# A graph-transformer kernel: reload, additions, norm and node projection joined in one stage by groups of five tiles

## What is computed

```python
# end of layer 0: x = x + mixture(layernorm(x)), the mixture returns tokens + shares
out = tokens                                   # the normed rows
for e in range(E):                             # 8 experts, the best two of a token count
    h = gelu(tokens @ w1[e] + b1[e]); y = h @ w2[e] + b2[e]
    out = out + combine[:, e:e + 1] * y
# start of layer 1
xn = layernorm(x)
hid = relu((xn[src] + edge_attr) @ W1 + b1)    # 40000 edges
```

## Time and profile before

| | us |
|---|---|
| median of 3 runs | 1409.33 (1406.69 to 1414.96) |
| the profiled execution | 1415.98 |
| its span | 1414.0 |
| busy PE / DVE / ACT / POOL | 1169.0 / 754.9 / 454.0 / 595.6 |
| mean granted clock of PE | 0.922 |

### The profile page before, as it was taken

One profiled execution on the slowest core, in us unless ns is written; L12 is line 12 of the kernel. 1 busy time (PEld: TensorE's weight loads), 2 busy tenths in 40 slices (PEclk: granted clock), 3 DMA queues, 4 the chain that ended last, 5 costly groups with the idle time before them and its releaser, 6 DMA issues. The chain is left out here.

```text
span 1414.0 us, 22751 instructions
## 1 busy us (share of the span) xinstructions
PE 1169.0 (83%) x7588; PEld 921.5 (65%) x7588; DVE 754.9 (53%) x2376; ACT 454.0 (32%) x916; POOL 595.6 (42%) x698
## 2 busy tenths in 40 slices
PE   3777789876972899617999999999999869966997
PEld 2677779443641677416878888888888645535886
DVE  5999981276578344384545555454356431252332
ACT  2477770331321332111324333333333233221110
POOL 3366640003121677402776676766667000003442
PEclk9899999997965899959999999999999989987999
DMA  5000000410025233365666666656565056576551
GB/s 126 1 2 2 2 2 2 107 12 1 0 71 192 78 98 99 92 161 156 199 175 191 183 198 181 188 180 190 176 192 180 6 171 186 117 159 206 172 177 53
DMA packets 97276, 165.62 MB, mean 117 GB/s; under 512 B 15506, under 2 KB 59182, under 8 KB 96774
## 3 DMA queue, kind: packets, MB, share of 16 engines
q1 hardware_dynamic: 71669, 90.69, 22.5%
q0 software_dynamic: 25488, 73.39, 17.9%
HBM read 138.40 MB, written 27.63 MB: 117 GB/s over the span
## 5 line engine op out<-in xcount | busy, mean ns | idle before, releaser
L2266 POOL DMA_INDIRECT em_gathered<-edge_table,el_which x313 | 301.7, 964 | 132.1 <-issue 74.2
L2278 PE MATMUL em_projected<-em_w,em_attr 128*128 128x256 f32 x1252 | 283.1, 384 | 7.6 <-PEq L1897 7.6
L2278 PEld LDWEIGHTS em_projected<-em_w,em_attr 128*128 128x128 f32 x1252 | 240.4, 193 | 42.5 <-issue 9.9
L2356 DVE TENSOR_TENSOR em_hidden<-em_projected,em_gathered 128x512 f32<-128x512 f32 (+1 forms) x157 | 108.3, 690 | 205.2 <-PE em_projected L2278 127.3
L2378 ACT ACTIVATE em_hidden<-em_hidden 128x512 f32<-128x512 f32 (+1 forms) x157 | 98.7, 628 | 271.5 <-DVE em_hidden L2356 271.4
L434 POOL TENSOR_SCALAR nm_hot_a<-nm_order,ek_places 128x125 bf16<-128x125 int16 x150 | 99.7, 673 | 51.1 <-PE nm_banks L558 47.7
L446 DVE TENSOR_SCALAR nm_hot_key<-nm_key_order,ek_keys 128x100 bf16<-128x100 int16 x500 | 118.4, 263 | 0.0
L2689 POOL DMA_INDIRECT oe_hidden<-oe_table,oo_node x27 | 25.9, 959 | 179.4 <-DMA oe_table<-state 130.0
L2761 PE MATMUL oe_banks<-oe_wd,xn_T 128*128 x432 | 98.1, 381 | 0.0
L445 DVE TENSOR_SCALAR nm_hot_a<-nm_order,ek_places 128x125 bf16<-128x125 int16 x350 | 94.6, 272 | 0.0
L2761 PEld LDWEIGHTS oe_banks<-oe_wd,xn_T 128*128 128x128 f32 x432 | 80.7, 192 | 9.8
(11 more groups left out here) (482 smaller groups left out, 2267.0 us busy)
## 6 DMA issues: line engine op xcount, KB each, us to landing
em_attr<-in_edge_attr_sets SPq DMA_DIRECT2D x156, 256.0 KB, 3.6
oe_table<-state SPq DMA_DIRECT2D x20, 448.0 KB
oe_wd<-in_ffn_Wd SPq DMA_DIRECT2D x8, 1024.0 KB
em_gathered<-edge_table,el_which POOLq DMA_INDIRECT x313, 3.6
mx_w<-in_ffn_w SPq DMA_DIRECT2D x16, 256.0 KB
oe_table<-state SPq DMA_DIRECT2D x1, 2248.8 KB
state<-in_x SPq DMA_DIRECT2D x5, 448.0 KB
state<-in_x SPq DMA_DIRECT2D x1, 2240.0 KB
```

What stands on the lines that cost most here:

```text
L2266: nc.gpsimd.indirect_dma_start(out=gathered[:, n % GATHERED, :], out_offset=None, in_=table, in_offset=bass.IndirectOffsetOnAxis(ap=lanes. ...
L2278: last = nc.tensor.matmul(projected[:, k % BANKS, n % 2, :], attr[:, k % ATTR_RING, (n % 2 * KB + f) * 128:(n % 2 * KB + f + 1) * 128], w1 ...
L2356: nc.vector.tensor_tensor(pair_slots(k), projected[:, k % BANKS, 0:width, :], gathered[:, at:at + width, :], ALU.add).then_inc(pre_ready, 1)
```

## The change

The reload and the additions leave the mixture's block; `normalise_to_first` becomes `answers_to_first`, which does them together with norm and projection, in four groups of five tiles (`PARTS`, `SIZE`).

- The first addition is split: ACT multiplies the first answer by its share in place (`weight`, L1972 of the changed kernel), POOL adds it to x (L1898), DVE adds the second answer as before (`add_second`, L1905).
- Statistics, variance and root are worked out per group. DVE normalises a group one group late: additions and statistics of group g, its variance, then the norm of group g - 1.
- The bias of the projection is added by PE, by a matmul of one row of ones with one row of the bias (L1949). ACT copies the projection out of PSUM (`keep`, L1980), three tiles behind the turn (L1984). DVE's copy is gone.
- SP issues the answers' loads, the attributes', the weights', clears, and only then stores the table, in four stores of five tiles.
- `hidden_sum`, which the edge stage fills later, now also takes the second answers; it, the shares and `answers` are made earlier for that.

The core of the diff (the removed lines of the mixture are L1697 to L1701 and L1854 to L1869 above, those of the old stage L1880 to L1968):

```diff
-def normalise_to_first(p, c, A, x, xn, xn_T, w, b, attr, attr_loaded, table, others, done):
+def answers_to_first(p, c, A, x, xn, xn_T, w, b, shares, answers, second, attr, attr_loaded, table, others, done):
-    BANKS, PARTS = 4, 5
+    BANKS, PARTS = 4, 4
     SIZE = TILES // PARTS
+    answer = [xn[:, :, 0:DIM], second[:]]
...
             @block.sync
             def _(sp):
+                for q in range(CHUNKS):
+                    for n in range(2):
+                        load_rows(sp, answer[n][:, q * 4:(q + 1) * 4, :],
+                                  answers[n * NODES + q * CHUNK:n * NODES + (q + 1) * CHUNK, :]
+                                  .rearrange("(t p) d -> p t d", p=P), answered[n][q])
                 for k in range(ATTR_RING):
                     load_attributes(sp, A, attr, attr_loaded, k)
-                for q in range(PARTS):
...
                 others.sync(sp)
                 clear(sp, done)
+                for g in range(PARTS):
+                    sp.wait_ge(kept, (g + 1) * SIZE)
+                    load_rows(sp, table[g * SIZE * P:(g + 1) * SIZE * P, :].rearrange("(t p) d -> p t d", p=P),
+                              rows[:, g * SIZE:(g + 1) * SIZE, :], stored)
                 sp.wait_ge(stored, 32 * PARTS)
+
+            @block.gpsimd
+            def _(pool):
+                for t in range(TILES):
+                    pool.wait_ge(weighted, t + 1)
+                    nc.gpsimd.tensor_tensor(x[:, t, :], x[:, t, :], answer[0][:, t, :], ALU.add).then_inc(joined, 1)

             @block.vector
             def _(dve):
+                def add_second(t):
+                    dve.wait_ge(answered[1][t // 4], 32)
+                    dve.wait_ge(joined, t + 1)
+                    nc.vector.scalar_tensor_tensor(x[:, t, :], answer[1][:, t, :], shares[1][:, t:t + 1], x[:, t, :],
+                                                   ALU.mult, ALU.add).then_inc(added, 1)
...
+                for g in range(PARTS):
+                    for t in tiles_of(g):
+                        add_second(t)
+                        if t % SIZE:
+                            measure(t - 1)
+                    measure(t)
+                    find_var(g)
+                    if g:
+                        normalise(g - 1)
+                normalise(PARTS - 1)
...
+                    nc.tensor.matmul(projected[:, t % BANKS, 0:DIM], c.ones[0:1, :P], b[0:1, :], start=True, stop=False)
                     for k in range(KB):
                         last = nc.tensor.matmul(projected[:, t % BANKS, 0:DIM], xn_T[:, k, t * P:(t + 1) * P], w[:, k, :],
-                                                start=(k == 0), stop=(k == KB - 1))
+                                                start=False, stop=(k == KB - 1))
...
             @block.scalar
             def _(act):
+                def weight(t):
+                    act.wait_ge(answered[0][t // 4], 32)
+                    nc.scalar.activation(answer[0][:, t, :], answer[0][:, t, :], ACT.Copy, scale=shares[0][:, t:t + 1]).then_inc(weighted, 1)
...
+                for g in range(PARTS + 2):
+                    if g < PARTS:
+                        for t in tiles_of(g):
+                            weight(t)
+                    if 1 <= g <= PARTS:
+                        root(g - 1)
+                    if g >= 2:
+                        for t in tiles_of(g - 2):
+                            turn(t)
+                for t in range(TILES - 3, TILES):
+                    keep(t)
```

More of the change, by code:

```diff
@@ L1625, in tensor_steps, with mixture @@
         last.then_inc(self.found, 1)
-def mixture(p, c, A, state, x, xn, xn_T, first_w, first_b):
+def mixture(p, c, A, state, x, xn, xn_T, first_w, first_b, shares, answers):
     nc = p.nc
@@ new lines, in measure, with find_var @@
+                def measure(t):
+                    dve.wait_ge(added, t + 1)
+                    nc.vector.bn_stats(c.stats[:, t * 6:(t + 1) * 6], x[:, t, :]).then_inc(measured, 1)
+                def find_var(g):
+                    dve.wait_ge(measured, (g + 1) * SIZE)
+                    nc.vector.tensor_tensor(half[:, g], s[:, g, 1, :], s[:, g, 4, :], ALU.subtract)
+                    nc.vector.tensor_tensor(mean[:, g], s[:, g, 1, :], s[:, g, 4, :], ALU.add)
+                    chain.tick(nc.vector.tensor_tensor(var[:, g], s[:, g, 2, :], s[:, g, 5, :], ALU.add))
+                    chain.wait(dve)
+                    nc.vector.tensor_scalar(mean[:, g], mean[:, g], 0.5, None, ALU.mult)
+                    chain.tick(nc.vector.scalar_tensor_tensor(half[:, g], half[:, g], 0.25, half[:, g], ALU.mult, ALU.mult))
+                    chain.wait(dve)
+                    chain.tick(nc.vector.scalar_tensor_tensor(var[:, g], var[:, g], 1.0 / DIM, half[:, g], ALU.mult, ALU.add))
+                    chain.wait(dve)
+                    nc.vector.tensor_scalar(var[:, g], var[:, g], LN_EPS, None, ALU.add).then_inc(var_ready, 1)
@@ L1961, in _, with root, keep, turn @@
             def _(act):
-                act.wait_ge(var_ready, 1)
-                nc.scalar.activation(std[:], var[:], ACT.Sqrt).then_inc(std_ready, 1)
-                for t in range(TILES):
+                def weight(t):
+                    act.wait_ge(answered[0][t // 4], 32)
+                    nc.scalar.activation(answer[0][:, t, :], answer[0][:, t, :], ACT.Copy, scale=shares[0][:, t:t + 1]).then_inc(weighted, 1)
+                def root(g):
+                    act.wait_ge(var_ready, g + 1)
+                    nc.scalar.activation(std[:, g], var[:, g], ACT.Sqrt).then_inc(std_ready, 1)
+                def keep(t):
+                    act.wait_ge(ready, t + 1)
+                    nc.scalar.activation(rows[:, t, :], projected[:, t % BANKS, 0:DIM], ACT.Copy).then_inc(kept, 1)
+                def turn(t):
                     act.wait_ge(transposed, t + 1)
@@ L2583, in layer1 @@
             attr_loaded = [p.sem(f"em_attr_loaded{u}") for u in range(ATTR_RING)]
[L2584 removed]
+            answers_to_first(p, c, A, x, xn, xn_T, w1, b1, shares, answers, hidden_sum, attr, attr_loaded, table, w, done)
             p.reuse(done)
@@ L2924, in graph_layers @@
         first_b = p.sb("em_b1", [P, DIM], scope=graph)
-        mixture(p, c, A, state, x, xn, xn_T, first_w, first_b)
+        hidden_sum = p.sb("hidden_sum", [P, TILES, DIM], scope=graph)
+        shares = [p.sb(f"shares{n}", [P, TILES], scope=graph) for n in range(2)]
+        answers = nc.dram_tensor("mx_answers", [2 * NODES, DIM], F32).ap()
+        mixture(p, c, A, state, x, xn, xn_T, first_w, first_b, shares, answers)
     if upto >= 3:
-        layer1(p, c, A, x, xn, xn_T, lanes, in_degree, first_w, first_b)
+        layer1(p, c, A, x, xn, xn_T, lanes, in_degree, first_w, first_b, shares, answers, hidden_sum)
 def laid_out(i):
```

73 lines of the change are left out of this document (17 added, 56 removed).

## The result

| | before | after |
|---|---|---|
| median | 1409.62 us | 1446.67 us (1445.9 to 1448.13) |
| ratio | | 1.0256, 95% interval 1.0233 to 1.028 |
| span of the profiled execution | 1414.0 | 1444.7 |
| busy PE | 1169.0 | 1215.9 |
| mean granted clock of PE | 0.922 | 0.905 |

The change made the kernel 37 us slower. The forecast was 1402.2, its range ended at 1409. Four points of each trace say where the time is: POOL's last indirect DMA of the mixture is issued, PE begins the first transpose of the stage, the last copy out of PSUM begins, the edge stage's first matmul begins.

The account below looks back on a forecast made before the run. The stretch was taken as bound in turn by loads and VectorE, TensorE, then SP's list. Gains of 4.2 us at PE's end and 2.9 at SP's made 7.1, from median 1409.33 to 1402.2 us; range 1396.5 to 1409.

Parts of the forecast that it names:

- Bias on PE: Projection: the one-row matmul adds 0.43 us, PE's tile goes from 1.08 to 1.51, taking back 8.6 us of 14.6.
- Rival C: Norm and projection: PE works in shorter pieces, its clock stays at 1.2 GHz, up to 1427.6 us; chance 0.06.
- Reload: Answers' loads move behind the mixture's block end, which costs 0.3 us; what is lost at 593 is won at 626.
- Additions: Answer additions: POOL and DVE take turns, 1.0 us a tile for the pair; PE starts at 614.6, not 629.25.
- rival A: Additions: POOL always goes before DVE, PE starts at 617.9, 2.7 us gained, 1406.6; chance 0.28 including nothing moving.
- Groups: Norm stage: group 2 is normalised from 631.4, PE has run out at 630.5, a wait of 1.3 us.
- SP's end: Last copy to edge stage: clears before stores leave 4.1 us and 0.1 of hand-over, for 7.1; 2.9 us gained.
- Sum: Mixture's end to edge stage: 7.1 us gained, 4.2 at PE's end and 2.9 at SP's; chance 0.47.

Follow-up runs that it names:

- e11: Changed kernel with the bias over 125 rows, the first two chunks loaded early and both additions on VectorE: ratio 0.9953 to the kernel before.
- e8: Changed kernel with the bias matmul over 125 rows and the first two of five chunks' loads issued inside the mixture's block: ratio 0.9958 to the kernel before.
- e2: Changed kernel with the bias matmul over 125 rows in place of one: ratio 1.0017 to the kernel before.
- e14: Changed kernel with the bias over 125 rows in tiles 0 to 9 and one row in tiles 10 to 19: ratio 1.0028 to the kernel before.
- e6: Changed kernel with the bias added by GpSimd to the copied rows, none on PE: ratio 1.0007 to the kernel before.
- e1: Changed kernel without the bias matmul, so its projection lacks the bias: ratio 0.9987 to the kernel before.
- e17: e11 with groups normalised after three tiles of the next, ScalarE's roots reordered, and 34 full-width matmuls ahead of the first transpose: ratio 0.9958 to the kernel before.
- e18: e17 with 16 more full-width matmuls behind the last projection: ratio 0.9934 to the kernel before.

## Why the prediction was wrong

*Bias on PE: the step that failed.* It says "the rows don't count, the columns do", from one 1-row record of 385 ns beside records of 384. For the duration of a lone record that is right, and with 125 rows the bias costs the 0.43 us forecast. But the row I read stood in a stage whose clock was already up, and it was one record, not one in every tile. Neither what it does to the clock, nor the steps around it (0.57 us a tile at half clock, 0.38 at full) is in such a row. Size: the bias was priced at 0.43 us a tile and cost 2.48 (3.56 less 1.08); from first transpose to last copy it was 71.5 us, forecast 35.1, and with 125 rows 34.3. Why few rows keep the clock down stays open: the runs show that they do.

*Rival C* named what came, a clock that stays at 1.2 GHz, and had 0.06 and the wrong reasons. The waits at group ends and the transposes are in the run with 125 rows too, where the clock rose; the part of its "for" that held was "one-row" matmuls. It gave the end of the last copy at 675.5; 690.93 came, 15.4 us later, of which 4.5 are the late start (619.06 against 614.6) and some 11 are 20 x 0.57. My argument against it, that the clock rose before "of the same mixture of work", was the mistake: the mixture was the one thing that the edit changed. By the rule of the Trainium skill that I weighed there (TensorE: Matmul & The Clock Gate, "PE-mode transpose"), transposes do not engage the full clock. The runs agree with the earlier trace rows and not with it: transposes and full-width projections alone, in the run without bias, had the clock at 1.00 from 3.5 us behind the first transpose.

*Reload: the other step that failed.* "One such end costs 0.3 us" was read at 626, at this very block's end, when POOL's drain had been over for 26 us. Moved to 591, the same end has the drain in it. "What is lost at 593 is won at 626" took the two for alike: 6.8 us by the trace, nearly the whole gain forecast.

*Additions.* From the first load to the first transpose 21.6 us, forecast 20.9: right. But this was luck in part: the term was argued from a collision, and that was mild. DVE's twenty additions in after took 0.46 to 0.98 us, and none the 1.5 or more that would have spoken for rival A; without any sharing, in the run e11, the first transpose comes as early (24.1 us against 25.5 from the last DMA).

*Groups.* One wait of 1.3 us at group 2: in the run e8 it is 1.03, at that place. In after PE is so slow that it doesn't occur.

*SP's end.* 4.2 us from the end of the last copy to the edge stage, measured 4.4 (690.93 to 695.37), and by itself, in the old order, 3 us of gain. Right.

*Sum.* With the bias over 125 rows and two chunks loaded early (e8) the forecast's mechanism is there: 0.9958 for 0.995, and 64.4 us from last DMA to edge stage, where the forecast's times give 63.1.

## What to carry to other kernels

Before a small matmul is put into a stage that TensorE bounds, ask how many of its rows it uses, not only how many columns it streams: here the same sum over 125 rows, all but one of them times zero, cost 0.43 us a tile, and over 1, 32 or 64 rows 2.5. When work is moved across a block's end, look at what each engine has to finish at that end, above all one that has issued its own DMAs; an end that costs 0.3 us at one place can cost 7 at another. And before reordering in-order lists, follow the whole loop through the engines: an early start that hangs weights behind turns made the period of a group longer than any engine's work.

## What the runs showed of the hardware

- Narrow matmuls (1, 32, 64 rows of contraction), two records to four full-width ones and two transposes, went with a granted clock of 0.50 for 70 us at a PE busy all the time; with 125 rows it rose, 4.1 us after the first transpose in e2. Once it was 1.00, one-row ones left it there for 17 us (e14).
- Each costs more than its columns: 0.38 us a tile at full clock, 0.57 at half.
- GpSimd's drain at the end of a block, counted from the end of its last instruction, differs with what it did there, and is the same in all twenty traces: 7.75 us at the mixture's end, behind indirect DMAs (the record is 9.38 long), 8.97 at the end of the edge stage, behind its 313 (the record is 10.7 to 19.4 long, over gathers that were still queued), and 0.07 behind additions. Where it had nothing to do, at the end of the norm stage of before, the record is 0.04 us.
- A pause of 4.9 us in TensorE's work took its clock down. A pause of 3.28 did in e6 and did not in e1; 2.8 in e17 did, 3.56 and 1.31 in e18 did not. So the length of a pause alone doesn't tell.
- Beside additions of GpSimd's, a two-input operation of VectorE's took 0.61 us for 0.47 on 125x256, and 0.69 for 0.16 on 125x5 (e8).
